# Attention scores from whole float32 operands in two row tiles of 64, in a fused decoder layer

## The reference

```python
x = x + gated_recurrence(layernorm(x))                      # stage A: z, h, scan, gate
q, k, v = layernorm(x) @ Wq + bq, ctx @ Wk + bk, ctx @ Wv + bv   # 16 heads of 32
scores = einsum('bhqd,bhkd->bhqk', q, k) / sqrt(32)         # causal: query row < key is masked
x = x + (softmax(scores) @ v) @ Wo + bo                     # stage B
x = x + mixture_of_experts(layernorm(x))                    # stage C: 4 experts, top 2
```

## Time and profile before

| | us |
|---|---|
| median of 3 runs (1182.05 to 1183.07) | 1182.75 |
| the profiled execution | 1185.1 |
| its span, first to last instruction | 1183.3 |
| stage B in that span (about 327 to 717) | 390 |
| PE busy in stage B | 374.5 |
| ACT busy in stage B | 268.0 |
| DVE busy in stage B | 293.9 |

### The profile page before, as it was taken

How to read it: one execution, slowest core, us unless ns; L and a number is a source line. 1 busy time by engine, 2 the same in 40 slices (tenths; PEclk the granted TensorE clock), 3 DMA queues, 4 the chain that set the end, 5 groups by cost and what they waited for, 6 DMA issues and landing times.

```text
span 1183.3 us, 24275 instructions
## 1 busy us (share of the span) xinstructions
PE 1127.1 (95%) x6017; PEld 930.4 (79%) x6018; DVE 906.2 (77%) x2161; ACT 714.1 (60%) x2080; POOL 442.8 (37%) x390
## 2 busy tenths in 40 slices
PE   6999999999989999999999988889999999999993
PEld 5888888888877788787887777777888888888882
DVE  6888888887775677878778866768777777777774
ACT  5223333233377767768676633767777777777773
POOL 3000000000043324545536353556655555555543
PEclk9999999999999999999999988999999999999998
DMA  8544544345420314133143388885554444444443
GB/s 259 165 148 151 204 160 168 134 168 187 167 103 1 90 54 143 55 90 98 46 143 90 126 230 220 230 228 103 83 85 84 80 84 84 80 84 84 80 65 43
DMA packets 95317, 144.76 MB, mean 122 GB/s; under 512 B 20865, under 2 KB 37429, under 8 KB 94608
## 3 DMA queue, kind: packets, MB, share of 16 engines
q1 hardware_dynamic: 77194, 105.78, 28.7%
q0 software_dynamic: 17216, 35.73, 17.2%
q10 hardware_dynamic: 837, 2.41, 0.6%
HBM read 82.69 MB, written 64.76 MB: 125 GB/s over the span
## 4 chain that ended last, share of the span: by engine, by line
PE 77%; DMA 9%; DVE 4%; issue 3%; ACT 3%; POOL 2%; SPq 1%; DVEq 0%; POOLq 0%; ACTq 0%
PE banks L1122 26%; PE banks L707 21%; PE banks L772 7%; PE banks L919 5%; DMA out<-rows,scatter_rows 5%; PE banks L897 4%; PE banks L884 3%; PE banks L1150 2%; PE banks L1134 2%; ACT rows L1331 2%; PE banks L908 2%; PE banks L940 2%; DMA rows<-slot_table 2%; PE banks L745 1%; DMA xf_rows<-rows 1%
## 5 line engine op out<-in xcount | busy, mean ns | idle before, releaser
L1122 PE MATMUL banks<-operands 128*128 x1608 | 389.6, 397 | 14.3 <-DVE operands L1599 7.9
L1122 PEld LDWEIGHTS banks<-operands 128*128 128x128 f32 x1608 | 298.8, 190 | 77.7 <-DVE operands L1599 9.6
L707 PE MATMUL banks<-operands 128*128 128x512 f32 (+2 forms) x1224 | 292.1, 394 | 3.6 <-DVE operands L1599 3.6
L707 PEld LDWEIGHTS banks<-operands 128*128 128x128 f32 (+1 forms) x1224 | 225.9, 192 | 47.8 <-DVE operands L1599 3.7
L1599 DVE TENSOR_TENSOR operands<-banks,operands 128x512 fp32r<-128x512 f32 (+1 forms) x232 | 157.1, 685 | 28.1 <-ACT operands L1214 24.8
L1214 ACT ACTIVATE operands<-banks 128x512 fp32r<-128x512 f32 (+1 forms) x232 | 136.3, 596 | 66.5 <-PE banks L798 33.1
L1331 ACT ACTIVATE rows<-banks,score_shift 128x77 f32<-128x77 f32 x512 | 158.5, 337 | 13.2 <-DVE score_shift L1820 13.0
L1214 ACT ACTIVATE operands<-rows 128x512 fp32r<-128x512 f32 (+2 forms) x77 | 54.0, 710 | 163.3 <-DVE rows L1670 139.2
L1524 ACT ACTIVATE banks<-banks,param_cols 128x128 f32<-128x128 f32 x268 | 99.2, 430 | 79.1 <-PE banks L1150 79.1
L2643 POOL DMA_INDIRECT out<-rows,scatter_rows x67 | 106.4, 1588 | 107.2 <-DVE rows L2389 67.3
L2562 POOL TENSOR_TENSOR rows<-rows,score_rec 128x1232 f32<-128x1232 f32 x32 | 72.8, 2276 | 147.7 <-DVE score_rec L1828 147.7
(11 more groups left out here) (180 smaller groups left out, 1683.5 us busy)
## 6 DMA issues: line engine op xcount, KB each, us to landing
expert_parts<-operands SPq DMA_DIRECT2D x32, 512.0 KB, 3.0
operands<-expert_parts SPq DMA_DIRECT2D x8, 2048.0 KB, 11.4
rows<-in_x SPq DMA_DIRECT2D x8, 1024.0 KB, 5.4
rows<-in_L_ffn_W SPq DMA_DIRECT2D x32, 256.0 KB, 3.6
x_rows<-rows SPq DMA_DIRECT2D x8, 1024.0 KB, 4.3
rows<-x_rows SPq DMA_DIRECT2D x8, 1024.0 KB, 5.9
xf_rows<-rows SPq DMA_DIRECT2D x32, 256.0 KB, 2.3
out<-rows SPq DMA_DIRECT2D x32, 256.0 KB, 2.8
```

The source lines that it names most:

```text
L707: last = nc.tensor.matmul(dst, stationary(a, k), moving(b, k), start=(t == 0 and k == 0), stop=(t == len(terms) - 1 and k == n_k - 1))
L1122: last = nc.tensor.matmul(dst, stationary[:, a, k, :], weights[:, w, bass.ds(e, 1), a2, k, :].rearrange("p e f -> p (e f)"), start=False, ...
```

## The change

The scores are made from whole float32 queries and keys, without split parts:

- `kT`, `kblk` and `qT` are float32. `kblk` is 2 heads wide: 154 columns instead of 308; partitions 0 to 63 hold heads 0 and 1 of a group in their own blocks, partitions 64 to 127 heads 2 and 3.
- For each (m, j) there are two matmuls instead of three, one for each half g of the partitions: 64 rows, 128 stationary columns, 154 moving columns. Half g of tiles j = 2i and 2i + 1 goes to bank 4 + 2i + g, so the two halves write different banks. A masked tile gets two matmuls with the identity (128 rows, 154 columns of `mask_r`) behind them.
- `q_hi` on ACT is gone. `q_lo` on DVE becomes `q_rows`, one addition of the bias straight from the bank, which waits for PE instead of ACT. Its places in DVE's order are those of `q_lo`.
- `max_scores` reads the same 616 columns in the new order, and `exp_scores` looks its shift up accordingly.
- In the front, the keys are written once, by ACT; four DVE instructions go, the 8 DMAs become 4 of half the bytes in all, and POOL clears a quarter of the columns. The waits on `k_lo` are on `k_ready`, which ACT sets.

```diff
-        kblk = r_at(48, 2 * B * KC * GK).rearrange("p (a b m g) -> p a b m g", a=2, b=B, m=KC)
+        qT = nc.alloc_sbuf_tensor_at("queries_T", [P, KC, CH], F32, offset=r_base + 32 * 1024)
+        kblk = nc.alloc_sbuf_tensor_at("key_blocks", [P, B, KC, HK], F32, offset=r_base + 48 * 1024)
+        kT = nc.alloc_sbuf_tensor_at("keys_T", [P, B, KC, SK], F32, offset=r_base + 91 * 1024 + 256)
-        s_banks = ps[:, 4:8, 0:GK]
+        s_banks = ps[:, 4:8, 0:2 * HK].rearrange("p (i g) (j w) -> p i g j w", i=2, j=2)
...
-            sp.wait_ge(k_lo, KC)
+            sp.wait_ge(k_ready, KC)
             for hl in range(HPG):
-                rows = slice(hl * DH, (hl + 1) * DH)
-                for a in (HI, LO):
-                    sp.dma_start(kblk[rows, a, :, :, hl * SK:(hl + 1) * SK].bitcast(F32),
-                                 kT[rows, a].bitcast(F32)).then_inc(k_placed, 16)
+                rows, at = slice(hl * DH, (hl + 1) * DH), (hl % HPH) * SK
+                sp.dma_start(kblk[rows, :, :, at:at + SK], kT[rows, :, :, :]).then_inc(k_placed, 16)
...
                 for j in tiles:
-                    for t, (a, a2) in enumerate(TERMS):
-                        keys = kblk[:, a2, b, m, :]
-                        last = nc.tensor.matmul(s_banks[:, j, :], qT[:, a, m, j * P:(j + 1) * P], keys,
-                                                start=(t == 0), stop=(t == len(TERMS) - 1 and not masked(c, j)))
+                    for g in range(2):
+                        rows = slice(g * P // 2, (g + 1) * P // 2)
+                        last = nc.tensor.matmul(s_banks[:, j // 2, g, j % 2, :], qT[rows, m, j * P:(j + 1) * P],
+                                                kblk[rows, b, m, :], start=True, stop=not masked(c, j))
                     if masked(c, j):
-                        last = nc.tensor.matmul(s_banks[:, j, :], ident_r, mask_r, start=False, stop=True)
+                        for g in range(2):
+                            last = nc.tensor.matmul(s_banks[:, j // 2, g, j % 2, :], ident_r, mask_r, start=False,
+                                                    stop=True)
...
-            def q_hi(c, m):
-                act.wait_ge(mm_done, mm_num(c - 1, f"q{m}") + 1)
-                nc.scalar.activation(qT[:, HI, m, :], mb(c - 1, f"q{m}"), ACT.Identity,
-                                     bias=pcol[:, ROW_BQ + m:ROW_BQ + m + 1]).then_inc(qT_hi, 1)
...
-            def q_lo(c, m):
-                dve.wait_ge(qT_hi, 4 * c + m + 1)
-                V.scalar_tensor_tensor(qT[:, LO, m, :], mb(c - 1, f"q{m}"), pcol[:, ROW_BQ + m:ROW_BQ + m + 1],
-                                       qT[:, HI, m, :].bitcast(F32), ALU.add, ALU.subtract).then_inc(mm_read, 1)
+            def q_rows(c, m):
+                dve.wait_ge(mm_done, mm_num(c - 1, f"q{m}") + 1)
+                V.tensor_scalar(qT[:, m, :], mb(c - 1, f"q{m}"), pcol[:, ROW_BQ + m:ROW_BQ + m + 1], None,
+                                ALU.add).then_inc(mm_read, 1)
...
-            G.memset(kblk[:, :, :, :, :].rearrange("p a b m g -> p (a b m g)").bitcast(F32), 0.0).then_inc(pool_step, 1)
+            G.memset(kblk[:, :, :, :].rearrange("p b m g -> p (b m g)"), 0.0).then_inc(pool_step, 1)
```

## The result

| | before | after |
|---|---|---|
| median (lowest to highest), 5 runs each, us | 1182.75 (1181.83 to 1186.05) | 1192.69 (1189.70 to 1195.59) |
| the profiled execution / its span, us | 1185.1 / 1183.3 | 1189.7 / 1187.9 |
| mean granted clock of that execution | 0.988 | 0.981 |

The ratio after to before is 1.0089, 95% interval 1.0062 to 1.0116: +9.9 us where +3.9 was forecast. Slower was right, and the time lies in the range; the amount was off by 6 us, and a part of the argument fell that had been written off in half a sentence ("the clock has no part").

What follows compares the result with a forecast made beforehand. PE's list was taken to bound stage B. New calls at 57.4 us against 57.9, plus 5.4 for masks, made +4.9; less 1.0 hidden in the first turn, +3.9, so 1186.6 us from 1182.75, range 1179 to 1211.

Steps and rivals of the forecast that it cites:

- the clock has no part: In the total: the granted clock, 0.99 in stage B, adds nothing to the forecast change of +3.9 us.
- What bounds it: Stage B lasts as long as PE's list; relief of ACT and DVE is worth nothing to PE.
- One pass, two passes, halves together: Score call: whole float32 takes two passes, both array halves run side by side, so the body is 0.545 us.
- the entry: Start of each score call: emptying the array and loading 128 columns costs 0.21 us, bounds 0.13 and 0.32.
- Leaving: Behind score calls: leaving the row tiles costs 0.16 us in front of transposes, 0.21 in front of products.
- Masks: In 8 masked calls, leaving the tiles, two full-array matmuls and entering again add 0.67 us each, 5.4 us together.
- The first turn hides 1.0: In the first turn, PE's waits for POOL's normalise (0.47 and 1.06 us) cover 1.0 us of the masked calls.
- The front: Ahead of stage B: less DVE, POOL and DMA work, counted as 0, with a bound of -1.2 us.
- Sum at full clock: Whole program: +4.9 us on PE's list less 1.0 hidden gives +3.9 us.
- Strict order: Rival, 6%: matmuls start in list order, so a score call lasts 5 passes instead of 4; +8.3 us, 1195.
- loads one at a time: Rival, 10%: weight loads of the two row tiles share one path in score calls; +20.5 us, 1207.
- cheap switching: Rival, 16%: row tiles need no emptying, so entries and exits of score calls vanish; -19.0 us, 1164.

Runs made afterwards that it cites:

- half the dose: Kernel before with the unread row-tiled pair ahead of only 32 of the 64 score calls (m = 2 and 3): 1207.77 us, ratio 1.0179.
- the second series: The changed kernel unaltered, measured again over 6 runs beside the kernel before: 1202.86 us, ratio 1.0117.
- where it was filled: Changed kernel with four more unread 512-column products ahead of the last `attend` of each of six middle turns: 1201.78 us, ratio 1.016.
- merged calls: Mask-first kernel with score calls side by side, five row-tile visits a middle turn, not eight: 1219.32 us; with DVE's and ACT's lists reordered to avoid waits, 1208.14.

## Why the prediction was right in its sign and wrong in its size

- *What bounds it.* Right. The stage is PE's list; giving ACT its instruction back changed nothing, and the two largest waits stayed nearly as in the earlier trace rows.
- *One pass, two passes, halves together.* Right: 512 and 16 records, and a call of 0.72 us. The forecast's 0.545 + 0.21 = 0.755 was 0.035 too much, 2.2 us in 64 calls. Most of it sits in the body, 0.52 by the starts of the passes and not 0.545; the entry is 0.20 with 0.21 forecast. The entry of `attend` with 0.08 added for the wider load was thus a good row to go by.
- *Leaving.* Right, 0.16 in front of transposes and 0.2 in front of products.
- *Masks.* Mechanism right, 0.58 instead of 0.67 more: 0.7 us in 8 calls. That this part is real was shown by putting the mask first, which saved 0.40 a call.
- *The first turn hides 1.0.* Half right. The wait of 0.47 at 338 us is gone. That of 1.06 is there again with 1.04. The normalise it waits for is released by the transposes at 352.61 (354.00 after), ahead of the masked call, and PE is let go 5.11 us behind their start before and 5.10 after. Of PE's work between, the masked call takes 0.33 us more, and the call behind `attend` 0.32 less, as it no longer pays for leaving the column tiles. The cover hid the first as I had said, and swallowed the second, which I had counted as saved.
- *The front.* Counted as 0, with a bound of -1.2. The first score came 1.1 us later (327.4 and 328.6). In the nine profiles of the changed kernel and its variants it lies between 327.6 and 329.9, in the four of the kernel before and its variants between 327.3 and 327.9. So about 1 us seems lost ahead of stage B; where was not traced.
- *Sum at full clock.* Forecast +3.9. With the measured terms, and 0.5 hidden, it would be +1.5 (3.9 - 2.2 - 0.7 + 0.5); stage B measures -1.0 and +1.1 in two profiles, and the whole program's work +0.8. Within what these measurements can tell, the tiled scores cost what the old ones did.
- *"The clock has no part".* The step that failed, and more than the whole miss of 6 us. I read a clock of 0.99 in stage B and only one slow stretch at its end, and took it as given, because PE stays busy throughout. But the change swaps time in which columns stream for time in which the array empties and loads. The prediction had this in its own sum (0.3 us less streaming a call, 0.3 more switching) and took the two as equal; over stage B the count gives 16 us less streaming. The clock went with that: in three kernels made from before, with nothing but unread products added, it fell from 0.986 to 0.972, 0.974 and, with half the dose, 0.981; and without the tiles it came back to 0.984. In stage B of the profiled execution this is 10.3 us, and in the medians of the second series 15 of 16 us. The miss is smaller than that because the work came out some 3 to 5 us below the forecast. Two errors of opposite sign met, and that the time lies in the range is luck to that extent.
- *Idle time as the cause.* Not here. In the windows of the changed kernel 1.2 GHz came behind stretches in which a matmul was always in flight (5.00 of 5.00 us), and what stood there was short work, gate products, `attend` and score calls in a row. "TensorE: Matmul & The Clock Gate", Part 1, in the Trainium skill, puts a falling clock down to gaps in TensorE's work. By the profile's busy time these windows do not agree.
- *The rivals.* Strict order would have given 0.885 us a call, loads one at a time 1.075, and cheap switching 0.87 for the transposes behind; the chain excludes all three at these prices. None of them named the clock, and one should have: the earlier trace rows, with 0.99 and not 1.00 in stage B, shows that it can fall even in before.

What stays open: why the stretches begin at a turn's end, even where nothing was added or where it was filled; why merged calls lower the clock more than separate ones; and why two series of the same kernel lie at 0.979 and 0.974 (the record names the chip only for the second). The clock varies by execution for before as well (0.981 to 0.991), and each kernel has one profile, so a place where a stretch begins may be chance. Shown is that added time with next to no streaming lowers the clock, with tiles changed or not, and that whole float32 by itself hardly does (0.984 beside 0.986). That streaming columns keep the clock up is the reading that fits this and the count above; merging shows that how the short work is grouped counts too.

## What to carry to other kernels

On a kernel whose TensorE is busy nearly all the time, write down two sums for a change of TensorE's work: the time on its list at full clock, and how much of that time streams columns. If the second falls (here by tile changes and short products), stretches at 1.2 GHz can come even at 95% busy, so compare span times granted clock before you trust a sum. And in a view of the chain, a piece that is longer by one factor together with all its neighbours, with no wait, is the clock and not the piece.

## What the runs showed of the hardware that I had not expected

- Row tiles of 64 run side by side: 8 passes of 0.13 us add 0.72 us, and the passes of the two tiles start in pairs within 0.01 us. Entering and leaving cost the same as for column tiles (the transposes behind: 1.03 instead of 0.87 in both).
- The mean granted clock, with TensorE 94 to 97% busy in stage B, moved between 0.957 and 0.988. It was 0.984 or more where columns streamed for 0.81 to 0.83 of stage B by the estimate, and 0.981 or less at 0.76 to 0.78. 64 pairs of 4-column products, 0.34 us each in the chain, cost 21.5 us of work and another 17.5 us of clock.
- A product of whole float32 in 308 columns, two passes, costs 1.04 us for two tiles, and one in three fp32r products 0.84. The row tiles' 0.72 lies below both, and is used up by the 0.16 to 0.2 behind it.
